# Two-layer network on one core: the product behind layer one's convolution in three terms of rounded halves, running sums in place, new places

## What is computed

```python
avg = jnp.cumsum(x, axis=1) / jnp.arange(1, l + 1)        # running mean over the tokens
ci = avg.reshape(b, l, H, d).transpose(0, 2, 1, 3)...     # 16 heads
pc = ci @ W_pe + b_pe
energy = stt + jax.nn.sigmoid(gate) * dyn
w = jax.nn.softmax(energy, axis=-1)                       # 31 weights for each token and head
...
for kk in range(K):
    out = out + w[:, :, kk:kk + 1] * padded[:, kk:kk + l, :]
conv_loc = out...reshape(b, l, d_model)
v = conv_loc @ W_fc.T + residual
v = (v - mu) / jnp.sqrt(var + EPS) * gamma + beta
...
h = jax.nn.relu(jnp.einsum('bsh,hi->bsi', hidden_states, W1) + b1)
return jnp.einsum('bsi,ih->bsh', h, W2) + b2              # perceptron, 256 to 1024 to 256
```

## Time and profile before

| | |
|---|---|
| time, three executions | 3524.27, 3524.38, 3525.11 us; median 3524.38 |
| profiled execution | 3523.81 us, of it 3522.0 us span |
| TensorE busy | 3263.8 us (93%) |
| VectorE, ScalarE, GpSimd busy | 2644.6, 2070.7, 1257.1 us |
| chain that ended last | TensorE 82%, VectorE 8%, ScalarE 3% |
| mean granted clock of TensorE | 0.96 of full speed |
| layer one | from 1989 us on |

### The profile page before, as it was taken

The page is one execution under the profiler, slowest core; times in us unless marked ns, Lnnn a source line. Parts: engine busy times, 40 slices in busy tenths (PEclk is TensorE's granted clock), DMA queues, the critical chain, the costliest instruction groups (busy, mean ns, idle before and its releaser), DMA issues.

```text
span 3522.0 us, 66894 instructions
## 1 busy us (share of the span) xinstructions
PE 3263.8 (93%) x24906; PEld 2755.0 (78%) x24906; DVE 2644.6 (75%) x6117; ACT 2070.7 (59%) x4047; POOL 1257.1 (36%) x1080
## 2 busy tenths in 40 slices
PE   6999999999993399999999459999999999999999
PEld 4888888888872299999999447888888888888888
DVE  5888888888877755555555378888888888888884
ACT  4667776677753355665555345555555555555554
POOL 1333333333230356665665333333223322333320
PEclk9999999999995599999999779999999999999999
DMA  5232333222211344444443365565566666666551
GB/s 177 100 100 87 113 107 106 76 66 86 68 43 70 69 102 106 105 102 98 105 95 80 81 122 118 121 125 123 126 127 128 128 123 127 126 127 127 126 102 41
DMA packets 745537, 366.07 MB, mean 104 GB/s; under 512 B 551190, under 2 KB 695774, under 8 KB 745086
## 3 DMA queue, kind: packets, MB, share of 16 engines
q1 hardware_dynamic: 716542, 318.78, 36.9%
q0 software_dynamic: 28672, 43.02, 6.8%
HBM read 224.73 MB, written 135.92 MB: 102 GB/s over the span
## 4 chain that ended last, share of the span: by engine, by line
PE 82%; DVE 8%; ACT 3%; issue 2%; DMA 2%; POOL 2%; SPq 1%; POOLq 0%; ACTq 0%; DVEq 0%
PE bank L1437 10%; PE bank L2044 10%; PE bank L2058 10%; PE bank L1423 10%; PE bank L838 9%; PE bank L818 9%; PE bank L2015 7%; PE bank L127 5%; PE bank L1994 3%; PE bank L2026 3%; PE bank L795 2%; DVE x L720 2%; DVE stats L631 1%; PE bank L1989 1%; PE bank L831 1%
## 5 line engine op out<-in xcount | busy, mean ns | idle before, releaser
L1353 DVE TENSOR_TENSOR hidden_low<-bank,hidden_high 128x512 fp32r<-128x512 f32 x256 | 176.4, 690 | 254.6 <-ACT hidden_high L1124 146.2
L838 PE MATMUL bank<-w_high,gT_low 128*128 128x256 f32 x1024 | 314.4, 307 | 1.9 <-DVE gT_low L710 1.9
L594 ACT ACTIVATE bank<-bank,b 128x512 f32<-128x512 f32 x256 | 168.6, 659 | 242.6 <-PE bank L818 239.5
L1805 ACT ACTIVATE bank<-bank,l_b 128x512 f32<-128x512 f32 x256 | 168.8, 660 | 239.9 <-PE bank L2044 239.7
L1117 ACT ACTIVATE bank<-bank,fc_bias 128x512 f32<-128x512 f32 x256 | 169.6, 662 | 237.8 <-PE bank L1423 227.1
L2058 PE MATMUL bank<-l_w_high,l_hidden_low 128*128 128x256 f32 x1024 | 302.9, 296 | 0.0
L2015 PE MATMUL bank<-bandT,window 128*32 128x96 f32 x5632 | 269.9, 344 | 24.8 <-DMA bandT<-bands 19.6
L838 PE MATMUL bank<-w_low,gT_high 128*128 128x256 f32 x1024 | 289.2, 282 | 0.0
L838 PE MATMUL bank<-w_high,gT_high 128*128 128x256 f32 x1024 | 289.1, 282 | 0.0
L2058 PE MATMUL bank<-l_w_high,l_hidden_high 128*128 128x256 f32 x1024 | 285.8, 279 | 0.0
L2058 PE MATMUL bank<-l_w_low,l_hidden_high 128*128 128x256 f32 x1024 | 285.7, 279 | 0.0
(11 more groups left out here) (315 smaller groups left out, 10619.6 us busy)
## 6 DMA issues: line engine op xcount, KB each, us to landing
bandT<-bands SPq DMA_DIRECT2D x352, 240.0 KB, 3.8
fc_full<-in_L_ffn_fc_wT SPq DMA_DIRECT2D x32, 1024.0 KB
bands<-zeros SPq DMA_DIRECT2D x22, 768.0 KB, 7.4
x<-in_L_attn_x SPq DMA_DIRECT2D x32, 512.0 KB, 6.0
moe_output<-zeros SPq DMA_DIRECT2D x32, 512.0 KB, 6.2
x_after_retention<-x SPq DMA_DIRECT2D x32, 512.0 KB, 3.0
moe_input_and_gates<-xn SPq DMA_DIRECT2D x32, 512.0 KB, 4.6
x<-x_after_retention SPq DMA_DIRECT2D x32, 512.0 KB, 5.6
```

The source lines that it names most:

```text
L838: m = pe.matmul(out, x, w, start=False, stop=f == KF - 1 and j == 2 and c % 2 == 1)
L1353: v.tensor_tensor(t.hidden.low[:, n % SLICES, :], K.banks[t.bank["expand", i, f, 0]][:, :], t.hidden.high[:, n % SLICES, :], ALU.subtract) ...
```

## The change

1. `w_fc` becomes a pair, high and low. It is loaded whole into the first buffer of `v`, rounded by ScalarE and split by VectorE in the step `prepare`, once.
2. A new step `round_mix` stands ahead of `mix`, for each chunk: ScalarE writes `mixT.high`, the rounded copy of the chunk's part of `convT`, and GpSimd writes `mixT.low`, the difference. There is one buffer `mixT`. ScalarE's rounding waits for the copies of the convolution and for the end of the mix before; the product waits for `mix_low`. The copies into `convT` now wait for `mix_low` of an older chunk where they waited for its mix.
3. `mix` multiplies in three terms: six products of 128x256 in place of two in float32. The transposes stay.
4. The tile `sums` (4 KB a partition) is gone: the scan writes into `avgT` and the factor is applied there; the last column goes into `carry` before that, by one copy of 128x1 for each of two pieces of the first half.
5. All places of layer one, the times in `BANKS_D` and one place of layer zero are new. The first expansion stands at 36.24 instead of 33.2, the first mix at 22.1 instead of 19.06, the first `turn_in` at 12.08 instead of 9.

```diff
+           "mix_high": ("ret_product", 64), "mix_low": ("h1T", 64)}
...
-    ... "root_mid": 27.25, ...
+    ... "root_mid": 28, ...
...
-    "mix": (19.06, 20.4, 21.9, 24.8, 26.2, 27.7, 30.6, 31.43), ...
+    "round_mix": (21.38, 21.88, 23.69, 27.12, 28.31, 30.02, 32.86, 33.75), "mix": (22.1, 23.44, 24.94, 27.76, 29.24, 31.06, 33.64, 34.47),
...
-EXPAND_D = 33.2
+EXPAND_D = 36.24
...
-    t.w_fc = K.tile(ctx, "w_fc", [P, KD, D])
+    t.w_fc = K.split_tile(ctx, "w_fc", [P, KD, D])
...
+    t.w_fc_full = t.v[0][:, 0:KD, :]
...
-    t.sums = K.tile(ctx, "sums", [P, KD, BANK])
+    t.carry = K.tile(ctx, "carry", [P, KD])
+    t.mixT = K.split_ring(ctx, "mixT", 1, [P, KD, P])
...
+        elif name == "round_mix":
+            (ch,) = args
+            n, place = t.C * b + ch, ch * P % t.CIRCLE
+            e.wait_ge(*K.later("mix_high", n + 1))
+            e.tensor_tensor(t.mixT[n % 1].low[:, :, :], t.convT[:, :, place:place + P], t.mixT[n % 1].high[:, :, :], ALU.subtract).then_inc(K.later("mix_low")[0], 1)
...
+        elif name == "prepare" and b == 0:
+            e.wait_ge(s("d_weights"), t.loads)
+            e.copy(t.w_fc.high[:, :, :], t.w_fc_full).then_inc(s("scalar_setup"), 1)
...
             if before:
-                e.wait_ge(s("mixed"), before)
+                e.wait_ge(*K.later("mix_low", before))
...
+        elif name == "round_mix":
+            (ch,) = args
+            n, place = C * b + ch, ch * P % t.CIRCLE
+            e.wait_ge(s("convT"), NT * b + -(-(ch + 1) * P // TT))
+            if n >= 1:
+                e.wait_ge(s("mixed"), n - 0)
+            e.copy(t.mixT[n % 1].high[:, :, :], t.convT[:, :, place:place + P]).then_inc(K.later("mix_high")[0], 1)
...
+        v.wait_ge(*K.setup("scalar", "w_fc_high"))
+        v.tensor_tensor(t.w_fc.low[:, :, :], t.w_fc_full, t.w_fc.high[:, :, :], ALU.subtract).then_inc(s("vector_setup"), 1)
...
-            sums, tokens = t.sums[:, k, :], slice(half * BANK, (half + 1) * BANK)
+            sums, tokens = t.avgT[b % 2][:, k, PAD + half * BANK:PAD + (half + 1) * BANK], slice(half * BANK, (half + 1) * BANK)
...
-            v.tensor_tensor(t.avgT[b % 2][:, k, PAD + half * BANK:PAD + (half + 1) * BANK], sums, t.per_count[:, tokens], ALU.mult).then_inc(s("avgT"), 1)
+            if half == 0:
+                v.tensor_copy(t.carry[:, k:k + 1], sums[:, BANK - 1:BANK]).then_inc(step, c.up())
+                v.wait_ge(step, c.n)
+            v.tensor_tensor(sums, sums, t.per_count[:, tokens], ALU.mult).then_inc(s("avgT"), 1)
...
-            place = ch * P % t.CIRCLE
-            pe.wait_ge(s("convT"), NT * b + -(-(ch + 1) * P // TT))
...
+            pe.wait_ge(*K.later("mix_low", n + 1))
             for k in range(KD):
-                m = pe.matmul(bank[:, 0:D], t.convT[:, k, place:place + P], t.w_fc[:, k, :], start=False, stop=k == KD - 1)
+                for j, (x, w) in enumerate(t.mixT[n % 1][:, k, :].pairs(t.w_fc[:, k, :])):
+                    m = pe.matmul(bank[:, 0:D], x, w, start=False, stop=k == KD - 1 and j == 2)
```

More of the change, by code:

```diff
@@ L1463 @@
 BANKS_D = {
[L1464 to L1465 removed]
+    "turn_in": (2, 0.27), "kernel_product": (2, 0.67), "window_turn": (1, 0.48), "convolve": (1, 0.51), "mix": (1, 0.77), "turn_mid": (2, 0.1),
+    "l1_expand": (1, 1.79),
 }
```

39 lines of the change are left out of this document (20 added, 19 removed).

## The result

| | kernel before | kernel after |
|---|---|---|
| median of the runs | 3524.32 us (4 runs, 3523.26 to 3525.11) | 3550.31 us (4 runs, 3548.88 to 3552.09) |
| ratio, 95% interval | 1 | 1.0075 (1.0063 to 1.0088) |
| profiled execution, its span | 3523.81, 3522.0 us | 3551.15, 3549.4 us |
| first product with `out_bias` in layer one | 2138.61 us | 2142.82 us |
| one batch in the middle part | 89.98 us | 91.71 us |

The change made the kernel slower by 26 us; I had forecast 16 us faster.

What follows compares the result with a forecast made beforehand. TensorE's own work was taken to bound layer one's middle part. Product -19.6, neighbours +3.9, banks -3.0 and opening +2.5 gave -16.2 us, from 3524.4 to 3508 us; range 3495 to 3531.

Steps and rivals of the forecast that it cites:

- The only wait of TensorE in the middle part: Layer one, 2160 to 3450 us: TensorE waits only 6.7 us, so each microsecond taken from its work shortens the span.
- The new wait: Ahead of each mix's six products: rounding and subtraction, some 1.2 us a chunk, fit beside TensorE's work; 0 in the middle part.
- VectorE: nothing on the path: Two carry copies of some 0.15 us a batch bring VectorE from 77.0 to 77.3 of 88.4 us; no cost.
- The product: Mix on TensorE: six rounded products cost 0.70 us instead of 0.87, saving 0.17 us a chunk, -19.6 us over 115 chunks.
- the neighbours: Different blocks side by side on TensorE in the new places: 0.27 us a batch, +3.9 us (-0.1 to +11).
- Banks: TensorE's 0.48 us bank wait once a batch goes, another pair becomes close: -3 us, between -6.7 and +3.6.
- Opening: Start of layer one: earlier VectorE work and exposed chains of the first mixes, +2.5 us (-4 to +12).
- End: End of the program: as many places behind the last mix as before, so 0.
- The slower one: Rival: rounding and subtraction come late for mixes, 1.2 us per bare chunk; two of eight give 3543 us; chance 0.18.
- The one on VectorE and GpSimd: Rival: GpSimd's new subtractions and VectorE hold each other, +7 to +17 us, 3515 to 3525; chance 0.16 shared with the opening.
- L1891's mean: Sign in the profile: this VectorE step, mean 0.957 us before, should average at most 1.2 us after if the forecast held.

Runs made afterwards that it cites:

- f4: Kernel before with one part of the change alone: running sums in `avgT`, the two carry copies and the multiplication in place; 3529.2 us, ratio 1.0014.
- e3: Kernel before, old arithmetic, with only the new places, expansion places and bank times; 3556.4 us, ratio 1.0093.
- f1: Changed kernel with the chain of the first half batch's running means (`norm_in`, `turn_in`, `average`) moved earlier; 3539.0 us, ratio 1.0043.
- h1: f1 with the first half batch's two running means moved earlier, around the last energy step and ahead of chunk 3's centering; 3548.2 us, ratio 1.0064.
- f2: e2 with GpSimd's subtraction cut from 128x256 to 128x2 from the second chunk on; 3525.8 us, ratio 1.0004.
- i2: i1 with GpSimd's subtraction cut from 128x256 to 128x2 from the second chunk on; 3503.6 us, ratio 0.9942.
- e2: New arithmetic in the kernel before's places and bank times, with `round_mix` added and mix 7 moved to 31.9; 3555.2 us, ratio 1.0091.
- i1: h1 with x3's statistics moved behind VectorE's `o` step and ScalarE's normalisation of x3 behind a window copy, first half batch; 3520.5 us, ratio 0.9990.
- g3: Changed kernel with GpSimd's subtraction cut from 128x256 to 128x2 from the second chunk on; 3549.9 us, ratio 1.0074.
- f3: f1 with the low half's subtraction on VectorE instead of GpSimd, 0.12 places behind the rounding; 3654.3 us, ratio 1.0367.
- e1b: Changed kernel with `kernel_product` 0 moved back from 13.07 to 13.2, behind a convolution; 3540.3 us, ratio 1.0046.
- g1_late_result: f1 with VectorE's `result` step moved from 58.87 to 59.75, by mistake between the two running means; 3562.0 us, ratio 1.0104.
- h2_means_conv: h1 with the tenth convolution of a batch moved from 32.02 to 32.3, behind the next expansion; 3549.9 us, ratio 1.0077.

## Why the prediction was wrong, point by point

**"The only wait of TensorE in the middle part ... so the middle part ends when TensorE's own work ends."** True of the profile, and the step from it was too large. That 1283 of 1290 us are busy says that every chain fits, not by how much; f4 showed that one had no room at all.

**The new wait.** For the chain that the change adds (rounding, subtraction, mix) the prediction compared chain and distance, and was right: no wait for `mixT_low` in the middle part, 0.40 us for the rounding and 0.75 for the subtraction against 0.37 and 0.7. For the chains that the change only moves it compared banks alone. "All places anew" was the larger edit, and the pair `turn_in` 0 and `kernel_product` 0, with 0.99 places in the diff instead of 1.80, was not looked at. This is the step that failed: a term of +2.29 us x 14 = +32 us, and some 10 us of half clock behind it, stood in the sum as 0. e3 shows it without the new arithmetic. f1 and h1 show that moving the chain doesn't give the 32 us back by itself, for the reason of the next point.

**"VectorE: nothing on the path".** Wrong even with the old table. Carry copies counted as nothing cost 4.7 us (f4), the subtraction 29 us in the old places (f2) and 17 us in repaired ones (i2), in part through VectorE. The forecast took the 12 us that VectorE is idle in a batch for room. They are not: its order is fixed, and of the 171 us that it was idle from 2190 to 3440 us in the kernel before, it waited 140 us for GpSimd and ScalarE:

```profile
DVE top L1889 <- POOL energies L1716: 92.7, 83, 2.0
DVE energies L1883 <- ACT l_th L1755: 27.6, 42, 3.7
DVE total L1896 <- ACT energies L1763: 19.5, 28, 1.0
```

**The product.** Six records 0.117 us apart came, but the first, behind transposes in float32, took 0.20:

```profile
2366.28 0.44 PE L2049 MATMUL bank<-ident,h3T 128*128 128x128 f32 x2
2366.47 0.36 PE L2053 MATMUL bank<-w_fc_high,mixT_low 128*128 128x256 f32 x1
2366.67 0.28 PE L2053 MATMUL bank<-w_fc_low,mixT_high 128*128 128x256 f32 x1
2366.79 0.28 PE L2053 MATMUL bank<-w_fc_high,mixT_high 128*128 128x256 f32 x1
...
2367.25 0.40 PE L2071 MATMUL bank<-h4T_high,l_w_low 128*128 128x512 f32 x1
```

A chunk with its transposes takes 0.97 us (2366.28 to 2367.25) instead of 0.22 + 0.87 = 1.09, a saving of 0.12 where 0.17 was forecast; -14 us instead of -19.6. Eight chunks give -1.0 us a batch; to the -0.8 us found above +0.2 is missing, which would be the neighbours (+0.27 forecast), but that is a remainder and not measured. i2's batch without its wait, 88.86 - 0.38 = 88.5 us, comes near to the 88.7 that this gives (89.98 - 0.48 - 0.8).

**Banks.** The old wait of 0.48 us went wholly (-6.7, the better end). **Opening.** +4.2 us instead of +2.5, inside its range; TensorE's wait for bands grew from 19.6 to 26.9 us, and two waits for `mixT_low` came up, 3.4 us together. **End.** Unchanged, as said.

**The rivals.** The slower one had the right shape, a chain exposed, and the wrong chain: in the middle part of the changed kernel `mixT_low` was never late, in e2 and i1 it was, by 0.7 and 0.3 us a batch. The one on VectorE and GpSimd was real but priced for the wrong state: 0 in the changed kernel (g3), 17 to 29 us where no larger wait covers it, against the 7 to 17 forecast. Its sign, L1891's mean, even improved, from 0.957 to 0.675 us as L1915, because the meetings had moved to other lines (L1902, in the kernel before, had a mean of 1.016 us):

```profile
L1926 DVE TENSOR_TENSOR w<-energies,total 128x496 f32<-128x496 f32 x109 | 144.7, 1327 | 4.1 <-DVE total L1922 0.4
L1915 DVE TENSOR_TENSOR energies<-energies,top 128x496 f32<-128x496 f32 x110 | 74.3, 675 | 3.8
```

e3, which has no subtraction on GpSimd, had the same for w (1.303 us): which VectorE step meets which GpSimd step is a matter of places. The Trainium skill (SBUF — State Buffer, "Who interferes with whom") has the rule that a VectorE instruction with two inputs in SBUF contends with a GpSimd instruction that reads SBUF, and that one with at most one such input, outside the two-port modes, does not. By that rule the runs agree: L1907 (L1883 in the kernel before), whose second input is a bank, took 0.66 to 0.67 us on average in every kernel here and never more than 0.69, while f3's subtraction, with both inputs in SBUF, took up to 2.6.

## What to carry to other kernels

When a table of places changes, compare for every pair of producer and consumer the old distance with the new one, and each with the length of the chain between them, read from the trace; the chains that are only moved matter as much as those that are added. An engine at 86% in a fixed order may have no room: ask at which step of it the busiest engine starts just as it ends, since such a hold of 0.1 us is in no list of waits. A wait is removed for good only when the engine behind it has time left; until then it comes up elsewhere, as in e1b, h1 and i1.

## What the runs showed of the hardware

TensorE's granted clock fell to half with waits that I had not thought long enough to matter: with ten of fourteen waits of 2.29 us in the changed kernel, all thirteen of some 3 us (2.97 to 3.34) in the middle part of g1_late_result, eleven of fourteen of 1.9 us in e3_places_only, six of fourteen of 1.8 us in h1_means_first, one of fourteen of 1.75 us in h2_means_conv, and none of fourteen of 1.5 us in f1_early_chain. Waits of one length went both ways, so length alone does not decide it; what else does is not shown. Each such stretch cost about 1.0 us in the changed kernel, nearly half as much again as the wait itself.

A GpSimd subtraction of 0.75 us, eight times a batch, put 2.3 us a batch on VectorE and 1.1 us on the time (i1 against i2). TensorE waited for its result at one mix a batch, by 0.3 us; the rest of the 1.1 us came by way of other steps.
